# Query, key and value products of the second self attention: split fp32 operands in six matmuls, or unsplit fp32 operands in two

## The reference, cut to what matters

```python
def _L1_attn_ref(x, wq, bq, wk, bk, wv, bv, wo, bo, cos, sin):
    ...
    b, t, dm = x.shape                       # 8, 112, 256
    h, d = (NUM_HEADS, dm // NUM_HEADS)      # 16, 16
    xq = (x @ wq.T + bq).reshape(b, h, t, d)
    xk = (x @ wk.T + bk).reshape(b, h, t, d)
    xv = (x @ wv.T + bv).reshape(b, h, t, d)
    ...
    xq = xq * c + rot_half(xq) * s
    xk = xk * c + rot_half(xk) * s
    scores = jnp.einsum('bhqd,bhkd->bhqk', xq, xk) / np.sqrt(d)
    p = jax.nn.softmax(scores, axis=-1)
    o = jnp.einsum('bhqk,bhkd->bhqd', p, xv)
    ...
    return o @ wo.T + bo
x = x + _L1_attn_ref(_layernorm(x, axis=-1), ...)
```

## Time and profile before

| | before |
|---|---|
| median of 3 runs | 750.91 us |
| lowest, highest | 749.07, 752.61 us |
| profiled execution, its own time | 750.71 us |
| its span, first to last instruction | 748.9 us |
| PE busy / PEld busy | 544.8 us (73%) / 454.1 us (61%) |
| DVE / ACT / POOL busy | 474.0 / 295.2 / 204.4 us |
| granted TensorE clock, mean | 0.848 of full |

### The profile page before, as it was taken

How to read it: one execution, slowest core, us unless ns; L and a number is a source line. 1 busy time by engine, 2 the same in 40 slices (tenths; PEclk the granted TensorE clock), 3 DMA queues, 4 the chain that set the end, 5 groups by cost and what they waited for, 6 DMA issues and landing times.

```text
span 748.9 us, 9669 instructions
## 1 busy us (share of the span) xinstructions
PE 544.8 (73%) x3100; PEld 454.1 (61%) x3100; DVE 474.0 (63%) x1359; ACT 295.2 (39%) x738; POOL 204.4 (27%) x263
## 2 busy tenths in 40 slices
PE   7979973100003476999999999998999897759980
PEld 6955463000003455799999999985677555548870
DVE  5158679998999833647755554567777332854454
ACT  2377702000010216334554464327888333415520
POOL 5022500100002421203333331605443411145434
PEclk8999995655555678699999999999999999769995
DMA  5200121511000301201111100006001500115623
GB/s 160 98 2 29 26 28 36 142 21 15 0 8 27 115 24 57 91 1 57 57 57 57 57 1 1 1 1 183 1 2 50 163 0 0 50 49 159 145 95 110
DMA packets 42025, 40.78 MB, mean 54 GB/s; under 512 B 12132, under 2 KB 38248, under 8 KB 41864
## 3 DMA queue, kind: packets, MB, share of 16 engines
q1 hardware_dynamic: 36392, 25.23, 11.8%
q0 software_dynamic: 5584, 14.93, 7.4%
HBM read 31.50 MB, written 5.64 MB: 50 GB/s over the span
## 4 chain that ended last, share of the span: by engine, by line
PE 53%; DVE 26%; DMA 5%; issue 4%; SPq 4%; ACT 4%; POOL 3%; POOLq 0%; DVEq 0%; ACTq 0%
PE ps L1073 48%; DVE big L1653 6%; PE ps L1076 5%; DVE mtmp L1648 3%; DMA big<-in_ctx 3%; SPq L527 2%; POOL big L782 2%; SPq L545 1%; DVE rk L1875 1%; ACT big L800 1%; DVE rk L1874 1%; DVE big L1694 1%; DVE big L1695 1%; DVE big L1882 1%; SPq L523 1%
## 5 line engine op out<-in xcount | busy, mean ns | idle before, releaser
L1073 PE MATMUL ps<-big_split 128*112 128x256 f32 x768 | 95.1, 284 | 0.0
L1073 PEld LDWEIGHTS ps<-big_split 128*112 128x112 f32 x768 | 94.3, 178 | 0.6
L1073 PE MATMUL ps<-big 112*128 112x112 f32 (+5 forms) x432 | 86.6, 351 | 9.4 <-DMA big<-in_ctx 7.6
L1073 PE MATMUL ps<-ctxT_r_split,big_split 128*128 128x448 f32 (+2 forms) x352 | 81.5, 365 | 4.2 <-DVE N_r_split L1556 3.7
L1073 PE MATMUL ps<-ones,esel 8*112 8x1 f32 x2 | 0.5, 330 | 104.1 <-DVE esel L1718 104.1
L1805 DVE TENSOR_TENSOR big_split<-big,big_split 128x448 fp32r<-128x448 f32 x64 | 51.8, 838 | 37.0 <-ACT big L800 36.3
L703 POOL TENSOR_TENSOR big_split<-ctxT_r,big_split 128x2048 fp32r<-128x2048 f32 x8 | 40.6, 5072 | 121.8 <-ACT big_split L913 107.5
L1073 PEld LDWEIGHTS ps<-ctxT_r_split,big_split 128*128 128x128 f32 (+1 forms) x352 | 63.2, 191 | 10.6 <-issue 4.6
L1653 DVE TENSOR_TENSOR_SCAN big<-mtmp,big 32x47 f32<-32x47 f32 x248 | 62.6, 287 | 10.6 <-DMA big<-Vc_r 10.6
L1073 PEld LDWEIGHTS ps<-big 112*128 112x128 f32 (+4 forms) x432 | 58.6, 194 | 16.3 <-DMA big<-in_ctx 7.9
L1073 PEld LDWEIGHTS ps<-ones,esel 8*112 8x112 f32 x2 | 0.4, 279 | 104.5 <-DVE esel L1718 104.5
(11 more groups left out here) (246 smaller groups left out, 1140.0 us busy)
## 6 DMA issues: line engine op xcount, KB each, us to landing
ctxT_r<-in_L_ffn_W POOLq DMA_DIRECT2D x16, 512.0 KB, 4.9
big<-in_ctx SPq DMA_DIRECT2D x8, 750.0 KB
routed<-Vc_r SPq DMA_DIRECT2D x29, 128.0 KB
big<-in_L_ffn_Wg SPq DMA_DIRECT2D x16, 128.0 KB, 2.5
big<-in_L_ffn_Wu SPq DMA_DIRECT2D x16, 128.0 KB, 2.5
big<-in_L_ffn_Wd SPq DMA_DIRECT2D x16, 128.0 KB, 2.6
big<-big SPq DMA_DIRECT2D x42, 26.4 KB
X<-in_x SPq DMA_DIRECT2D x2, 448.0 KB, 4.9
```

Source lines behind the costliest of these rows:

```text
L1073: return nc.tensor.matmul(dst, lhsT, rhs, start=first, stop=last)
```

## The change

The tokens of norm 3 are no longer split: ACT copies the four banks into the fp32 tile NT and empties them (`ln_turned(3)`), and DVE's four subtractions go. The weights wT are no longer split: ACT's copy in step 13, with its two waits, and POOL's subtraction, with its wait, go. The six matmuls of each slot become two matmul calls on fp32 tiles. PE waits for `rope_ready` where it waited for `wt_lo_ready`, and for ACT where it waited for DVE. (The diff also defines two views of the split cross-attention tile a second time, the same as before, which changes nothing.)

```diff
-        ln_slots[3] = ring.take(*[dve] * 4)
+        ln_slots[3] = ring.take(*[act] * 4)
...
             for e in range(2, E0):
                 load_w0(e)
                 w0_lo(e)
-            pool.wait_ge(s["wt_hi_ready"], 1)
-            nc.gpsimd.tensor_tensor(wTs[:, 1].rearrange("p k (w n) -> p k w n", w=3), wT[:, :, 0:3, :],
-                                    wTs[:, 0].rearrange("p k (w n) -> p k w n", w=3), ALU.subtract)\
-                .then_inc(s["wt_lo_ready"], 1)
...
                     w0_hi(u // 2 + 1)
-                if u == 2 * E0 - 3:
-
-                    sc.wait_ge(s["w0_lo_ready"], E0)
-                    sc.wait_ge(s["rope_ready"], KD + 1)
-                    nc.scalar.activation(wTs[:, 0].rearrange("p k (w n) -> p k w n", w=3), wT[:, :, 0:3, :], ACT.Copy)\
-                        .then_inc(s["wt_hi_ready"], 1)
             ln_scale(3)
-            ln_hi(3, NTs3)
+            ln_turned(3)
...
             ln_turn(3)
 
-            pe.wait_ge(s["wt_lo_ready"], 1)
+            pe.wait_ge(s["rope_ready"], KD + 1)
             for i, slot in enumerate(r_qkv):
                 b = i // 2
                 cols = slice(0, 2 * D) if i % 2 == 0 else slice(2 * D, 3 * D)
-                wait_dve(ln_slots[3][KD * (b // HB) + KD - 1])
-                filled(split_mm(bank(slot)[0:T, 0:cols.stop - cols.start], lambda a, k: NTs3[a][:, k, tok(b)],
-                                lambda a, k: wTs[:, a, k, cols], KD))
+                wait_act(ln_slots[3][KD * (b // HB) + KD - 1])
+                dst = bank(slot)[0:T, 0:cols.stop - cols.start]
+                for k in range(KD):
+                    last = mm(dst, NT[:, k, tok(b)], wT[:, k].rearrange("p w n -> p (w n)")[:, cols], k == 0, k == KD - 1)
+                filled(last)
...
-            norm_lo_from_bank(3, NTs3)
             for i, slot in enumerate(r_qkv):
```

More of the change, by code:

```diff
@@ L235, in decoder_kernel @@
         assert KD * B * T <= (HB + 1) * S
+        NTs1 = [KcT_s[:, 2 * a * KD * B * T:(2 * a + 1) * KD * B * T].rearrange("p (k n) -> p k n", k=KD)
+                for a in range(2)]
+        assert KD * B * T <= (HB + 1) * S
         NTs3 = [big_s[:, o_h0 + a * KD * B * T:o_h0 + (a + 1) * KD * B * T].rearrange("p (k n) -> p k n", k=KD)
@@ L448, in decoder_kernel @@
                  "router_loaded", "wq1_loaded", "pc_shift", "wxa_loaded", "wxb_loaded", "out_stored", "mask_ready",
-                 "edge_ready", "norm_lo_ready", "w0_hi_ready", "w0_lo_ready", "hidden_lo_ready", "wt_hi_ready",
-                 "wt_lo_ready", "shared_hi_ready", "shared_lo_ready", "shared_loaded",
+                 "edge_ready", "norm_lo_ready", "w0_hi_ready", "w0_lo_ready", "hidden_lo_ready",
+                 "shared_hi_ready", "shared_lo_ready", "shared_loaded",
                  "order_ready", "normed_stored", "rank_in_ready", "places_ready", "tile_w_ready", "source_ready",
```

## The result

The changed kernel takes 754.75 us (median of 14 runs, 752.66 to 756.32) against 751.45 us for the kernel before (14 runs, 749.07 to 752.68): ratio 1.0045, 95% interval 1.0032 to 1.0058. That is 3.3 us more; forecast were 3.15 us and 0.42%, 753.9 us in a range of 751.8 to 756.4. The profiled execution has a span of 751.9 us and a mean granted clock of 0.849 (before: 748.9 and 0.848).

A forecast was written before the change was run, and what follows sets the result against it. The prediction took PE, busy without a break through the query, key and value products, as the bound; +3.8 us for fp32 products and -0.65 us for an earlier start took 750.71 to 753.9 us, range 751.8 to 756.4.

The forecast's parts named there:

- The path: Query, key and value products after norm 3: wholly on the path, each PE microsecond more there is one at the end.
- The prices: Same products: fp32 records at 429 ns (512 columns) and 216 ns (256), 20.64 us against 16.8, so +3.8 us.
- Rival (a): New products: fp32 passes run at the split pace, 232 and 118 ns, giving 744.5 us; chance 0.04.
- The start: First product waits for ACT's second copy, not DVE's second subtraction, starting at about 482.35 instead of 483.00: -0.65 us.
- my upper bound: Ahead of the first product: three semaphore waits might cost what today's gap costs, so an early-start gain of 0.
- What was priced at nothing: Dropped ACT weight copy (1.49 us), POOL subtraction (3.90 us) and DVE work elsewhere: in slack, worth nothing.
- The sum: Whole kernel: +3.8 - 0.65 = +3.15 us, 0.42% slower, from 750.71 to 753.9 us.
- (b): In or just behind the products' stage: another half-clock stretch costs 1.5 us, giving 755.4 us; chance 0.12.
- (c): Behind the stage: a wait for something that doesn't move swallows part of 3.15 us, giving 751 to 753; chance 0.07.

The follow-up runs named there:

- later start: The changed kernel with its first product waiting for ACT's fourth copy instead of its second; 755.31 us, ratio 1.0059 to the kernel before.
- reordered form: The kernel before with the split matmuls needing only the tokens' hi part put first; 748.23 us, ratio 0.9964, and again 746.94 us, 0.9946.
- query and key unsplit: The kernel before with query and key products on fp32 tiles, value products still split, tokens copied twice by ACT; 750.95 us, ratio 0.9999.

## Why the prediction was right

**The path.** The products lie wholly on it: right. The turn of QKV moved by what the stage grew, and taking 5.5 us out of the stage took 6.2 us out of the kernel, the rest being mostly a low stretch that it no longer met.

**The prices.** 216 ns was read and 429 ns worked out; the trace has both. 8 x (4 x 429 + 4 x 216) = 20.64 us, against 20.66 us in the chain. From the first product to the first turn of QKV, with the last add in it, the trace has 21.32 us against 17.52, +3.80. The Trainium skill's page "FP8 and Floating Point Precision", section "TensorE Precision Notes", counts four passes for true fp32; the estimate made from it was 20.8 us. The trace agrees in time, with 20.66 us, but shows two long records for each call and not four. Rival (a), fp32 records at the pace of the split ones, is out.

**The start.** -0.65 forecast; from the first turn of norm 3 to the first product the trace has 4.23 us against 4.89, -0.66. The later start and the reordered form confirm from both sides what it hangs on, ACT's copies after the change and DVE's subtraction before it. That the waits might cost what the gap costs, my upper bound, is out.

**What was priced at nothing** is worth nothing: putting ACT's and POOL's work back left the stage at 25.56 us. The 1.14 us for DVE's pair of adds was too much, as it is 0.94 in a row, but DVE was far from the limit here.

**The sum.** +3.14 us in the stage, +3.16 us from the first turn of norm 3 to the end of the trace, +3.3 us in the medians.

**The rivals.** Here the prediction was less good than its number. I gave (b), a changed clock, 0.12 and only one sign, in or just behind the stage, and (c), a delay taken up later, 0.07, looking for waits. The stages that are 0.84, 1.96 and 5.38 us longer end 1.0 to 2.4 us under the sum in their traces: a delay is often taken up later, and it is the clock of parts far behind that does most of it. That the sum held to 0.2 us is in part luck. It held because the kernel before and the changed one happen to meet two low stretches each, 62.07 and 62.02 us. Had the stage grown by 2 us instead of 3, the same working would have given +2 where query and key unsplit measured nothing.

**A better version.** The reordered split form beats both kernels: 746.94 and 748.23 us in two comparisons, ratios 0.9946 and 0.9964. Of its 2.7 to 4.1 us only 0.76 are its own, the closed gap; the rest is the clock in the cross attention, and 0.67 us of dummy work undid all but 0.6 us of it.

## What to carry to other kernels

Price a plain fp32 product by its own rows: here it is two records for each call, each nearly as long as two split passes over the same columns (216 against 118 ns, 429 against 232), so four plain records for D = 256 cost more than six split ones. The change saved matmuls and work on three engines and still lost, since only PE's time for the products was on the path.

For a change of under one per cent, look at the granted clock of every later part that stands at full and half clock in turn before trusting a sum, and move that part with dummy work before crediting the change with what is left over.

## What the runs showed of the hardware that I had not expected

A part of the program that wasn't changed, 100 us behind the change, took 62.07, 60.37 or 58.70 us, by how many stretches of 3.40 us at half clock it met, and a shift of 0.7 to 2 us of all that is ahead of it was enough to change the number. And less matmul work can slow what follows: in the trace with only the hi x hi products PE waited 2.63 us for DVE, the granted clock fell, and the next 48 transposes took 7.79 us instead of 4.82. The clock came back to full at 497.9 us, when PE had done nothing but transposes for 6.2 us. That the waiting is what made it fall is argued from the order of events in one execution.
